# Neighbour stage of a graph and mixture-of-experts kernel: gathered batches added in parts of four and three tiles, third routing one batch earlier

## The reference, cut to what matters

```python
agg = jnp.zeros_like(x).at[dst].set(x[src])        # the last edge of a node wins
h = jnp.concatenate((x, agg), axis=-1)
x = x + (h @ W.T + b)                              # x was layer-normed inside

logits = tokens @ router_w.T                       # tokens = layernorm(x)
probs = softmax(logits); rw, re = top_k(probs, 2)  # two experts a token
for e in range(8):
    out = out + combine[:, e:e+1] * (gelu(tokens @ w1[e] + b1[e]) @ w2[e] + b2[e])
x = x + out
```

## Time and profile before

| | us |
|---|---|
| device time, median of 3 runs | 1196.66 |
| lowest and highest of them | 1186.67 and 1199.59 |
| span of the profiled execution | 1180.7 |
| median less that span | 15.96 |

### The profile page before, as it was taken

The page is one execution under the profiler, slowest core; times in us unless marked ns, Lnnn a source line. Parts: engine busy times, 40 slices in busy tenths (PEclk is TensorE's granted clock), DMA queues, the critical chain, the costliest instruction groups (busy, mean ns, idle before and its releaser), DMA issues.

```text
span 1180.7 us, 28647 instructions
## 1 busy us (share of the span) xinstructions
PE 836.3 (71%) x9319; PEld 702.9 (60%) x9319; DVE 868.3 (74%) x1893; ACT 630.4 (53%) x1669; POOL 484.9 (41%) x527
## 2 busy tenths in 40 slices
PE   1599888887666862243444468888888888888886
PEld 1588887776555651132333256776766666767766
DVE  6999999995677764477688946776667666766666
ACT  3466666663444331264553345666666565666665
POOL 7000000004445556764650035555555555555554
PEclk9799999999888795555555789999999999999999
DMA  8800000003664444553551712222222222222220
GB/s 228 266 28 27 27 27 27 27 27 84 208 202 149 118 121 144 156 165 99 160 170 63 7 42 68 64 65 61 65 66 64 64 65 66 63 67 65 70 60 11
DMA packets 79211, 104.89 MB, mean 89 GB/s; under 512 B 22593, under 2 KB 64538, under 8 KB 78994
## 3 DMA queue, kind: packets, MB, share of 16 engines
q0 software_dynamic: 21408, 54.87, 16.6%
q1 hardware_dynamic: 57714, 48.76, 14.8%
HBM read 63.16 MB, written 44.01 MB: 91 GB/s over the span
## 4 chain that ended last, share of the span: by engine, by line
PE 31%; DVE 28%; issue 14%; another core or an unknown queue 12%; ACT 8%; DMA 3%; POOL 1%; ACTq 1%; DVEq 1%; SPq 1%; POOLq 0%
PE bank L983 12%; PE bank L997 9%; DVE arena L1099 7%; PE bank L786 6%; DVE arena L1082 5%; ACT arena L750 2%; PE bank L951 2%; PE bank L809 1%; ACT arena L711 1%; DVE bst L1300 1%; DVE arena L1283 1%; DVE big L1297 1%; POOL arena L517 1%; ACT arena L695 1%
## 5 line engine op out<-in xcount | busy, mean ns | idle before, releaser
L983 PE MATMUL bank<-arena,w1s 128*128 128x128 f16 x3000 | 211.2, 220 | 78.0 <-issue 69.1
L983 PEld LDWEIGHTS bank<-arena,w1s 128*128 x3000 | 177.8, 98 | 112.8 <-issue 109.8
L505 POOL DMA_INDIRECT arena<-key_rows,cid x98 | 94.8, 968 | 330.0 <-DVEq L1215 252.7
L750 ACT ACTIVATE arena<-bank,b1s 128x128 f32<-128x128 f32 x500 | 142.0, 368 | 155.6 <-remote 152.1
L532 POOL DMA_INDIRECT out<-arena,gidx x125 | 140.3, 1123 | 188.9 <-DVE arena L1438 149.5
L997 PE MATMUL bank<-w2s,arena 128*128 x1500 | 184.1, 272 | 1.4 <-DVE arena L1418 0.7
L521 POOL DMA_INDIRECT arena<-tok_rows,gidx x125 | 124.4, 995 | 107.4 <-DVE gidx L1407 69.4
L809 PE MATMUL bank<-wgs,arena 128*128 128x256 f16 x1176 | 160.0, 289 | 5.6 <-issue 5.4
L1433 DVE SCALAR_TENSOR_TENSOR arena<-bank,arena 128x256 f32<-128x256 f32 x125 | 60.1, 481 | 132.7 <-remote 129.5
L997 PEld LDWEIGHTS bank<-w2s,arena 128*128 128x128 f16 x1500 | 140.7, 98 | 17.8 <-issue 1.7
L809 PEld LDWEIGHTS bank<-wgs,arena 128*128 128x128 f16 x1176 | 121.7, 104 | 34.1 <-issue 8.6
(11 more groups left out here) (215 smaller groups left out, 1414.9 us busy)
## 6 DMA issues: line engine op xcount, KB each, us to landing
agg_rows<-arena SPq DMA_DIRECT2D x49, 256.0 KB
tok_rows<-arena SPq DMA_DIRECT2D x13, 896.0 KB
big<-x SPq DMA_DIRECT2D x5, 1792.0 KB, 14.1
arena<-w SPq DMA_DIRECT2D x16, 256.0 KB, 2.9
big<-x SPq DMA_DIRECT2D x6, 512.0 KB
arena<-tok_rows,gidx POOLq DMA_INDIRECT x125
out<-arena,gidx POOLq DMA_INDIRECT x125
arena<-key_rows,cid POOLq DMA_INDIRECT x98
```

Of the source, the lines that this page charges most:

```text
L505: gp.indirect_dma_start(er[:, b % 2, s, :], None, key_rows, bass.IndirectOffsetOnAxis(cid[:, t:t + 1], 0)).then_inc(er_full[b % 2], 16)
L750: last = sc.activation(h32[:, u % 2, at:at + P], bank[2 + u % 2][:, at:at + P], ACT.Gelu, bias=b1s[:, ds(e[x], 1), f], scale=1.0 / SCALE)
L983: last = mm(bank[2 + u % 2][:, at:at + P], parts[x, w, c, f], a[:, u % 4, c * P:(c + 1) * P], start=(n == 0), stop=(n == 5))
```

## The change

It does three things. The gathers of a batch of seven tiles count two semaphores, one for its first four tiles and one for its last three, and DVE adds, waits and takes statistics in those two parts; batches 13 and 14 are one part each. `pg_used` is counted right behind the second part's add. The routed ranges become 28, 28, 20 and 22 tiles where they were 28, 28, 28 and 14, and `route(2)` stands behind batch 11 where it stood behind batch 12; PE drains its logits that much earlier.

```diff
-ROUTED = [(n, min(RG, T - n)) for n in range(0, T, RG)]
+ROUTED = [(0, 28), (28, 28), (56, 20), (76, 22)]
...
+HALF = 4
...
-def gathered(n):
-    return 16 * sum(PIECES[k][1] for k in range(n % 2, n + 1, 2))
+def halves_of(n):
+    more = PIECES[n][1]
+    return [(0, min(HALF, more)), (HALF, more)][:2 if more > HALF else 1]
+
+
+def gathered(n, h):
+    return 16 * sum(b - a for k in range(n % 2, n + 1, 2) for a, b in halves_of(k)[h:h + 1])
...
-                                          bass.IndirectOffsetOnAxis(gat[:, t:t + 1], 0)).then_inc(pg_full[n % 2], 16)
+                                          bass.IndirectOffsetOnAxis(gat[:, t:t + 1], 0)
+                                          ).then_inc(pg_full[n % 2][s // HALF], 16)
...
-            early = turned(3 * RG)
+            early = turned(ROUTED[3][0])
...
-                dve.wait_ge(pg_full[n % 2], gathered(n))
-                step(ve.tensor_tensor(xs[:, of, :], xs[:, of, :], pg[:, n % 2, 0:more, :], ALU.add))
-                dve.sem_inc(pg_used, 1)
-                for s in range(more):
-                    last = ve.bn_stats(bst3[:, s, :], xs[:, first + s, :])
-                step(last)
+                for h, (a, b) in enumerate(halves_of(n)):
+                    rows = slice(first + a, first + b)
+                    dve.wait_ge(pg_full[n % 2][h], gathered(n, h))
+                    step(ve.tensor_tensor(xs[:, rows, :], xs[:, rows, :], pg[:, n % 2, a:b, :], ALU.add))
+                    if b == more:
+                        dve.sem_inc(pg_used, 1)
+                    for s in range(a, b):
+                        last = ve.bn_stats(bst3[:, s, :], xs[:, first + s, :])
+                    did.done(last)
+                did.settle()
...
-                if n == len(PIECES) - 3:
+                if n == len(PIECES) - 4:
                     low_turned(turned(first))
                     route(2)
```

More of the change, by code:

```diff
@@ L278, in gnn_moe @@
         s_b2, b2_scaled = sem("s_b2"), sem("b2_scaled")
-        pg_full = [sem("pg_full0"), sem("pg_full1")]
+        pg_full = [[sem(f"pg_full{k}{h}") for h in range(2)] for k in range(2)]
         pg_used = sem("pg_used")
@@ L878, in logit @@
                     t = first + h
-                    to = bank[LBANK[t // RG]][:, t % RG * E:(t % RG + 1) * E]
+                    c = max(n for n, (at, _) in enumerate(ROUTED) if at <= t)
+                    to = bank[LBANK[c]][:, (t - ROUTED[c][0]) * E:(t - ROUTED[c][0] + 1) * E]
                     k = 0
```

## The result

The changed kernel takes 1202.18 us (median of 22 runs, 1196.34 to 1207.92), the kernel before 1191.18 (22 runs on the same chip, 1186.66 to 1201.03). The medians differ by 11.0 us. The ratio is 1.0084 with a 95% interval of 1.0063 to 1.0105: the change costs 10 us (7.5 to 12.5), where the prediction had half a microsecond. The profiled execution of the changed kernel took 1201.76 us with a span of 1200.0, so only 1.8 us lie outside the span. The execution of the kernel before that was profiled (span 1180.7) had thus taken about 1182.5 us, quicker than any of the 22. Row against row the traces differ by 19.3 us, where the runs differ by 10. The 15.96 us that I had put around the span was for the greater part the quickness of that one execution.

The account below looks back on a forecast made before the run. The neighbour stage was taken as bound by a chain of DVE releases, POOL's gather runs and PE's gaps. Terms +3.4 - 2.25 + 1.2 - 1.85 = +0.5 us gave span 1181.2, plus 15.96 made 1197.2; range 1187 to 1206.

Parts of the forecast that it names:

- The ring with PE's gaps: Neighbour stage, 187 us: DVE releases, POOL gathers, PE falls short of instructions until POOL's run ends, then ACT and DVE continue.
- The gaps left as they are: PE's gaps in the neighbour stage: the sum let releases shift their ends but added or removed none, each 9 to 14 us.
- Later release: DVE's release to POOL comes 1.7 us later; for batches 3 and 6 that lies on the path, +3.4 us.
- The rival of the late release: Four late releases cost 6.8 us, DVE's extra work 1.5, routing in a gap 2: +8.5 us, 1205.2, chance 0.2.
- Shorter adds beside gathers: Shorter DVE adds hold POOL's gathers less: 0.75 us for each of three adds (batches 4, 5, 7), -2.25 us.
- DVE's own 0.30 a batch: The second add and step cost DVE 0.30 us per batch, counted for batches 8 to 11: +1.2 us.
- Earlier first part: First four tiles handled while three land, 2.4 us less in batches waiting for data; counted nothing, since PE's gaps swallow it.
- Third routing: Moved routing near the stage's end saves batch 12's data wait and a PE wait, less 0.30 for batch 12: -1.85 us.
- The 15.96 us around the span: Whole kernel: the median was taken to lie 15.96 us above the profiled span, added to the forecast span of 1181.2.
- a gap less: Rival: batch 1's work reaches PE before the first gap, so ACT's 13.51 us go; -10.7, near 1186.5, chance 0.12.

Follow-up runs that it names:

- e4: Kernel before with POOL's 98 neighbour-stage gathers replaced by plain loads that SyncE issues, choice of neighbour left out: 1135.0 us beside 1181.0, ratio 0.9602.
- e3: Changed kernel with both adds back to back, each behind its own wait, then the release, then all statistics: 1192.86 us beside 1181.0, ratio 1.0086.
- e1: Changed kernel with the routing put back (28, 28, 28, 14, third routing behind batch 12), parts kept: 1193.0 us beside 1181.0, ratio 1.0081.
- e11: Kernel before with its seven-tile add cut in two, back to back behind the one wait, on a quick chip: 993.86 us beside 999.5, ratio 0.9955.
- e12: Kernel before with its seven-tile add cut in two, back to back behind the one wait, on a chip with gaps: 1193.93 us beside 1192.3, ratio 1.0014.
- e2: Changed kernel with each batch of seven tiles as one part, moved routing kept: 1184.0 us beside 1181.0, ratio 1.0029.
- e5: Changed kernel with the routing put back and both semaphore waits ahead of one seven-tile add, on a quick chip: 1001.67 us beside 1000.4, ratio 1.0011.
- e10: Changed kernel with the routing put back and both semaphore waits ahead of one seven-tile add, quick chip again: 1001.1 us beside 999.5, ratio 1.0012.

## Why the prediction was right and wrong

The number was near, the effect wasn't. The range held 1202.2 and a change of under 1% was given 0.80, but I forecast half a microsecond and 10 were measured. Step by step:

- **The ring with PE's gaps** holds on the chips of the first runs. e4 shows that the gaps go with the gathers, and with them 46 us. That a gap ends when POOL's run ends, which I read from four of four, doesn't hold in the changed kernel: the first ends 5.1 us behind the run, two others inside one. The four were a choice even before. The long wait of the second run was 9.35 us and ended 0.4 us after the run's last gather began (535.15), and I took the short one behind it:

```profile
535.57 0.60 ACT L695 ACTIVATE arena<-bank 128x512 f16<-128x512 f32 x1 [9.35 <-remote]
538.53 0.60 ACT L695 ACTIVATE arena<-bank 128x512 f16<-128x512 f32 x1 [2.36 <-remote]
```

- **The gaps left as they are.** This is the step that failed. The sum moved the gaps with POOL's releases and gave none of them another length or another place in DVE's work; the moved gap had a price only in the rivals. The text did name the danger: a gap more or less is 9 to 14 us, more than all terms together. In the table the second routing stands 10.9 to 17.0 us behind the add of batch 9 in the four kernels with short adds, where it was 7.8.
- **Later release, +3.4, 1.7 us each.** It is 1.5 each (4.35 less 2.85). POOL's pauses before batches 5 and 8 grew by more, 4.8 and 2.7 us, since DVE itself was late. The price is open: e3 has the release back, is 5 to 6 us quicker than e1 and the changed kernel between batches 3 and 9, and by its time gains nothing. The rival of the late release gave 1205.2, nearer to the measured effect than the forecast, with a mechanism that alone can't carry it.
- **Shorter adds beside gathers, -2.25.** The relief is there, and larger: gathers take 96.2 us in sum against 102.6. Its value hangs on who waits. Where POOL sets the pace it is 5.7 us (e11); where PE's gaps do, the cut add stands at 1.0014 (e12), no gain. The Trainium skill, SBUF — State Buffer, section "SBUF: two separate sides", has the shared port pair held for the whole instruction. The prediction took from it that two adds hold a gather for their sum. That doesn't follow, for a lock held for one instruction can be free ahead of the next, and the trace agrees with the page: e12's gather ended 0.82 us behind the first add, as a gather did behind the one add of the earlier trace rows.
- **DVE's own 0.30 a batch, +1.2.** Where DVE doesn't wait, a batch of seven takes 8.02 us in the changed kernel (508.31 to 516.33) and took 7.83 (504.71 to 512.54), so it is 0.2.
- **Earlier first part, counted 0.** On the first three batches that was right: the stage gains nothing by it up to batch 3 (53.1 against 52.2), and the first gap swallows it. Further on it can't be told from the rest. By the ratios e1 and e3, which have it, cost 0.8 to 0.9%, and e12, which doesn't, 0.14% (-0.1 to 0.39); by the traces e3 and e12 lose the same nine microseconds at the same place.
- **Third routing, -1.85.** Its pieces were right to 0.05 us, and the whole was not found: e2 stands at +3.4 us with an interval from -0.2 to 7.1 (0.0029 of 1181). The wait for ACT's copy ahead of it was 2.52 in the changed kernel with 2.96 for the copy before that, and not 1.43 in all. The text put its start at 609.5 in one place and near 612 in another; its own sum has it at 610.
- **The 15.96 us around the span** were wrong by 14. The profiled execution was a quick one.

That the time fell inside the range is in part luck: the range was made wide for a gap less and for the late release, and what came is neither.

**What the runs leave open.** The times of the kernel before lie in groups some 10 us apart: on the first chip twelve of 22 between 1186.7 and 1191.3 and ten between 1194.7 and 1201.0; on the chip of e1 to e3 nineteen of 21 between 1177.5 and 1183.8 and two at 1191.6 and 1193.4; on the chip of e12 one at 1181.1, fifteen between 1189.0 and 1196.5 and one at 1198.9. The kernels with short adds are never in the lower group: all 22 runs of the change lie at 1196.3 or above, all sixteen of e1 and e3 at 1189.3 or above. Nine of the twelve of e2, with its one add, are at 1185.1 or below. Against the upper ten of the kernel before (their median is 1199.1) the change costs only 3 us. So I read it thus: the gap ahead of the second routing is what parts the groups, the change makes sure of it, and e12's chip had it already in the kernel before, so that e12 had little to lose. This is argued and not shown. The traces of before and e2 are of quick executions (about 1182.5 and 1180.3 us), and none was taken of the kernel before in its upper group. The edit of e12 never ran on a chip on which the kernel before is mostly in the lower group; that would settle it. Nor did the second semaphore alone (e5, e10) ever meet a chip with gaps. Settled are: the loss belongs to the parts (e1), the late release alone doesn't explain it (e3), and the moved routing has the smaller part at most (e2).

## What to carry to other kernels

Before costing a change by microseconds of an engine's work, find out whether the engine's idle time is that of a dependence or of missing instructions: rows that read "issue", one instruction at a time at even distances, look like the latter, and here work that was moved earlier into them only waited longer. Such a gap costs by what stands behind it: beside DVE's routing it was hidden, ahead of it it cost some 9 us. A short add beside indirect gathers gained 5.7 us where POOL set the pace and nothing that could be seen where it didn't, and the same edit gained on one chip and cost on the next, so a result of under 1% should be taken on more than one. Look at the single times as well: where they lie in groups, a trace shows one group and the median another. And the span of one profiled execution belongs beside that execution's own time, never beside a median.

## What the runs showed of the hardware

**Two sorts of chips.** One kernel takes 1181 to 1192 us on some chips and 1000 on others. The granted clock isn't the reason; the stretch of the experts, 125 tiles, in the changed kernel on a chip of either sort (us, busy us of PE, PEld, DVE, ACT and POOL, granted clock, DMA share, GB/s):

```profile
700.00:1190.00 490.00, 401.64 (x4744) 343.64 (x4745) 326.93 (x752) 311.13 (x876) 264.92 (x247) 0.98 0.22 62
```

```profile
610.00:980.00 370.00, 361.44 (x4729) 340.03 (x4730) 323.00 (x743) 317.69 (x876) 265.79 (x246) 0.99 0.29 82
```

The same instructions at the same clock take 120 us longer. Most of it (74 us) is PE without a releaser, in the groups of either page:

```profile
L991 PE MATMUL bank<-arena,w1s 128*128 128x128 f16 x3000 | 210.4, 221 | 81.5 <-issue 77.5
```

```profile
L991 PE MATMUL bank<-arena,w1s 128*128 128x128 f16 x3000 | 189.0, 220 | 4.8 <-issue 3.1
```

A matmul takes 0.22 us in both; the 3000 of them overlap less on the slower chip, which is another 21 us (210.4 less 189.0). This stretch, too, has indirect gathers and scatters of POOL (250 of them), so I read it as the same lack of instructions, which only the neighbour stage's runs (e4) tested. The Trainium skill, Runtime: NRT & Kernel Launch, section "Instruction fetch mechanics", has the fetch of the next block as mostly hidden. On the quick chips the trace agrees (3.1 us); on the others 77.5 us of PE's idle time in this line have no releaser. That this idle time is the fetch is my reading and not tested: the pages count 64 packets of an instruction queue in every execution and show no time for them.

**Even distances.** In the gaps PE's single matmuls start 0.7, 1.4, 2.1 or 2.8 us apart. In the first gap it is 0.7 to 2.1, mostly 1.4 or less, in the two kernels with one add a batch (before and e2) and mostly 2.1 to 2.8 in the four with two adds (the changed one, e1, e3, e12). It goes with the short adds and not with the early first part, which e12 doesn't have. I have no account of it.
